# Expert bias moved into the expert tiles, PSUM banks dealt anew, and the end of an iteration reordered, in a fused two-layer transformer kernel

## The reference, cut to what matters

```
gate_logits = x @ W_gate;  top_w, top_idx = top_k(gate_logits, 2);  top_w = softmax(top_w)
combine = sum over k of one_hot(top_idx) * top_w
for e in range(8):
    h = gelu(x @ W_in[e] + b_in[e])
    y = h @ W_out[e] + b_out[e]
    out = out + combine[..., e, None] * y
x = layernorm(x + out)
```

## Time and profile before

| | |
|---|---|
| median of 3 runs | 1523.08 us (1520.47 to 1523.33) |
| profiled execution, own time | 1521.35 us |
| its span, first to last instruction | 1519.7 us |
| PE busy | 1297.7 us, 85% |
| DVE, ACT, POOL busy | 917.5, 650.7, 614.7 us |
| softmax attention | 0 to 587 us |
| iterations 0 and 1 | 587 to 656 us |
| iterations 2 to 8 | 656 to 1240 us, PE busy 540.0 |
| last iteration | 1240 to 1317 us, PE busy 46.6 |
| hand-over to the experts | 1317 to 1341 us |
| expert tiles | 1341 to 1481 us, PE busy 136.7 |
| final norm | 1481 to 1519.7 us |

### The profile page before, as it was taken

The page is one execution under the profiler, slowest core; times in us unless marked ns, Lnnn a source line. Parts: engine busy times, 40 slices in busy tenths (PEclk is TensorE's granted clock), DMA queues, the critical chain, the costliest instruction groups (busy, mean ns, idle before and its releaser), DMA issues. The chain is left out here.

```text
span 1519.7 us, 34060 instructions
## 1 busy us (share of the span) xinstructions
PE 1297.7 (85%) x10704; PEld 745.3 (49%) x10705; DVE 917.5 (60%) x2055; ACT 650.7 (43%) x1290; POOL 614.7 (40%) x655
## 2 busy tenths in 40 slices
PE   6699999899999985998989999998989885499990
PEld 4243333333333332346565565646565553389990
DVE  6778887688887672155645646565645636445445
ACT  4065555555555564242524333242415221155553
POOL 7123232223232232035362827264463728235556
PEclk9599999999999997999999999999999998689995
DMA  6351111111111103030302203040402122132225
GB/s 196 101 186 38 37 37 51 40 47 37 35 38 50 44 14 102 8 82 6 97 9 57 52 26 83 7 102 7 102 5 59 34 91 61 39 111 68 66 58 168
DMA packets 88046, 93.09 MB, mean 61 GB/s; under 512 B 17192, under 2 KB 72368, under 8 KB 87856
## 3 DMA queue, kind: packets, MB, share of 16 engines
q1 hardware_dynamic: 73232, 74.39, 17.8%
q0 software_dynamic: 9184, 13.39, 2.9%
q10 hardware_dynamic: 5568, 4.53, 0.9%
HBM read 49.32 MB, written 22.63 MB: 47 GB/s over the span
## 5 line engine op out<-in xcount | busy, mean ns | idle before, releaser
L1307 ACT ACTIVATE arena<-banks 128x512 f32<-128x512 f32 x576 | 302.4, 599 | 239.2 <-PE banks L1222 237.7
L1354 DVE TENSOR_REDUCE arena<-banks 128x4 f32<-128x512 f32 (+3 forms) x336 | 343.8, 1055 | 89.8 <-PE banks L1200 85.8
L413 PE MATMUL banks<-arena,h 128*128 128x512 f32 x512 | 227.3, 594 | 2.6 <-ACTq L361 1.0
L1197 PE MATMUL banks<-arena 96*128 96x512 bf16 (+3 forms) x768 | 209.0, 341 | 20.8 <-DVE arena L1354 14.4
L1222 PE MATMUL banks<-arena 99*128 99x512 bf16 (+3 forms) x768 | 175.8, 328 | 16.4 <-ACT arena L1307 11.3
L1475 POOL TENSOR_SCALAR_AFFINE_SELECT arena<-arena 128x512 f32<-128x512 f32 x128 | 79.9, 636 | 229.2 <-ACT arena L1307 229.2
L1247 PE MATMUL banks<-arena 128*32 128x512 f32 (+3 forms) x1536 | 156.8, 496 | 15.7 <-POOL arena L1475 15.6
L413 PEld LDWEIGHTS banks<-arena,h 128*128 128x128 f32 x512 | 94.7, 190 | 110.3 <-issue 106.3
L1197 PEld LDWEIGHTS banks<-arena 96*128 96x128 bf16 x768 | 68.0, 100 | 158.7 <-DVE arena L1354 115.9
L429 POOL TENSOR_TENSOR arena<-arena 128x4 f32<-128x4 f32 x24 | 24.5, 1019 | 290.7 <-DVE arena L427 290.7
L502 POOL TENSOR_TENSOR arena<-arena 128x1024 f32<-128x1024 f32 x40 | 100.1, 2508 | 82.2 <-DVE arena L500 82.2
(11 more groups left out here) (168 smaller groups left out, 2019.8 us busy)
## 6 DMA issues: line engine op xcount, KB each, us to landing
arena<-arena SPq DMA_DIRECT2D x160, 128.0 KB, 2.3
arena<-q_parts SPq DMA_DIRECT2D x96, 96.0 KB
arena<-k_parts SPq DMA_DIRECT2D x288, 32.0 KB
arena<-rows SPq DMA_DIRECT2D x72, 65.0 KB
arena<-best SPq DMA_DIRECT2D x16, 256.0 KB, 4.5
k_parts<-arena SPq DMA_DIRECT2D x24, 128.0 KB, 2.8
q_parts<-arena POOLq DMA_DIRECT2D x18, 128.0 KB, 2.9
arena<-in_xT SPq DMA_DIRECT2D x8, 256.0 KB, 4.3
```

What stands on the lines that cost most here:

```text
L413: ins = nc.tensor.matmul(dst, l, r, start=(n == 0), stop=(n == len(pairs) - 1), skip_group_check=True)
L1197: ins = nc.tensor.matmul(dst, sq[p][0:MROW, h, qt * P:(qt + 1) * P], sk[p][0:MROW, h, k0:k0 + n], start=True, stop=not diag, skip_group_ch ...
L1307: nc.scalar.activation(pe_[:, s % NSLOT, :], score[s % NBANK], ACT.Exp, scale=SCALE0)\
L1354: nc.vector.tensor_reduce(mx[:, 1 if k0 else 0, qt, hs[0]:hs[-1] + 1], src, AX.X, ALU.max)\
```

## The change

The diff does four things.

- The bias leaves the iteration: picked, comb, turn_w, turned_w, bias, start and `acc` go. x3 itself is stored to `rest_d` right behind norm 3, from ACT's queue. `b_dn` is now laid out over all partitions and loaded beside `w_in`, so that each expert has 512 + 128 columns. `take_w` copies all 640 of them, a new DVE step `weigh` (one tile ahead) multiplies the 128 bias columns by the token weights, and `take_y` becomes a scalar_tensor_tensor that adds this product. `take_w` and `take_y` wait for `s_bias` too.
- The banks of the linear attention: `attend` takes its two `got` banks first and its two `grown` banks behind them, and one bank is skipped before `scores1(0)`. Now pv1 takes banks 6 and 7, freed by the masks of step 1; pv2 banks 4 and 5, freed by the masks of step 2; pv3 banks 0 and 1, freed by state1; the scores of step 3 banks 2 and 3, freed by state0.
- The end of the iteration: tile2(3) comes ahead of `choose`, and `route` (count on PE, place to weight on DVE) comes behind norm 2 and ahead of the scatters. down0 holds bank 0, count bank 1.
- The start: turn2 comes behind m = 2 instead of m = 1, and silu no longer waits for the bias of the iteration before.

```diff
         res = view([P, B, P])
-        acc = view([P, B, P])
         gated = view([P, 2, 512])
-        hid = [view([P, 4, 512]) for _ in range(2)]
-        w_in = view([P, NE, 512])
+        hid_both = view([P, 8 * 512])
+        hid = [hid_both[:, 2048 * i:2048 * i + 2048].rearrange("p (k t) -> p k t", k=4) for i in range(2)]
+        w_in = view([P, NE, 512 + C])
         stats = view([P, B, 8])
...
+            def skip_bank(self):
+                self.held.append(self.held[len(self.held) - 8])
+
             def pad_banks(self):
                 while len(self.held) % 8:
-                    self.held.append(self.held[len(self.held) - 8])
+                    self.skip_bank()
...
             for m in range(4):
-                if m == 2:
+                if m == 3:
                     tp.part = "rear"
...
                     bk, late["w1"][:, m * P:(m + 1) * P], xt1, start=True, stop=True))
-                tp.do("act", f"silu{m}", [f"up_a{m}", f"mul{m - 2}" if m >= 2 else (f"mul{m + 2}", 1), ("bias", 1)],
+                tp.do("act", f"silu{m}", [f"up_a{m}", f"mul{m - 2}" if m >= 2 else (f"mul{m + 2}", 1)],
                       lambda: nc.scalar.activation(gated[:, m % 2, :], bk, ACT.Silu, scale=late["s1"][:, m:m + 1]))
...
                 pr, half = n % 2, n // 2
-                got, *grown, other = [tp.bank() for i in range(4)]
-                got = [got, other]
+                got, grown = ([tp.bank() for i in range(2)] for j in range(2))
                 assert grown[0][0] % 8 < 7
...
+            tp.skip_bank()
             scores1(0)
...
             tp.part = "rear"
-            layernorm(tp, 3, "res3_3", res, x3, [("scatter7", 1), ("start", 1)])
+            layernorm(tp, 3, "res3_3", res, x3, [("scatter7", 1), ("stored", 1)])
             tp.do("act", "x3_again", ["norm3", ("scatter7", 1)], lambda: nc.scalar.copy(x3_rows[:, 1, :, 0:C], x3))
+            tp.do("act", "stored", ["norm3"], lambda: nc.scalar.dma_start(
+                rest_d[bass.ds(c, 1)].rearrange("c p b k -> p (c b) k"), x3), line="out")
...
                     wgt[:, 1, :], wgt[:, 1, :], wgt[:, 0, :], ALU.mult))
-                tp.do("dve", "picked", ["second", "onehot"], lambda: last(nc.vector.tensor_tensor(
-                    pick[:, i, :, :], chosen[:, B * i:B * i + B, :],
-                    wgt[:, i, :].rearrange("p (b o) -> p b o", o=1).to_broadcast([P, B, 8]), ALU.mult)
-                    for i in range(2)))
-                tp.do("dve", "comb", ["picked", ("turn_w", 1)], lambda: nc.vector.tensor_tensor(
-                    comb, pick[:, 0, :, :], pick[:, 1, :, :], ALU.add))
...
             turned(tp, 3, x3, x3T, [("gate", 1), "up_b3"])
-            choose()
             tp.part = "front"
...
             tp.part = "rear"
-            route()
+            choose()
             tp.part = "pre"
...
             tp.part = "rear"
+            route()
             for g in range(TOPK * B):
...
                     in_=x3_rows[:, g // B, g % B, :], in_offset=None), line="scat", apart=(g == 0))
-
-
-            tp.part = "rear"
-            k, bk, fr = tp.bank()
-            tp.do("pe", "turn_w", ["comb"] + fr, lambda: last(nc.tensor.transpose(
-                bk[0:8, t * P:(t + 1) * P], comb[:, t, :], ident[:, :]) for t in range(B)))
-            tp.do("act", "turned_w", ["turn_w", ("bias", 1), "mul3"], lambda: nc.scalar.copy(combT[0:8, :], bk[0:8, :]))
-            tp.free(k, "turned_w")
-
-            k, bk, fr = tp.bank()
-            tp.do("pe", "bias", ["turned_w"] + fr, lambda: last(nc.tensor.matmul(
-                bk[:, t * P:(t + 1) * P], combT[0:8, t * P:(t + 1) * P], late["b_dn"][0:8, :], start=True, stop=True)
-                for t in range(B)))
-            tp.do("dve", "start", ["bias", ("stored", 1)], lambda: nc.vector.tensor_tensor(
-                acc, bk.rearrange("p (b c) -> p b c", b=B), x3, ALU.add))
-            tp.free(k, "start")
-            tp.do("act", "stored", ["start"], lambda: nc.scalar.dma_start(
-                rest_d[bass.ds(c, 1)].rearrange("c p b k -> p (c b) k"), acc), line="out")
             tp.pad_banks()
...
             if me == "sp":
-                nc.sync.dma_start(w_in, a["w_in"].rearrange("e p m -> p e m")).then_inc(s_experts, 16)
+                nc.sync.dma_start(w_in[:, :, 0:512], a["w_in"].rearrange("e p m -> p e m")).then_inc(s_experts, 16)
+                nc.sync.dma_start(w_in[:, :, 512:512 + C], a["b_dn"]).then_inc(s_experts, 16)
                 for g in range(NE):
...
             if me in ("pe", "dve"):
-                e.wait_ge(s_experts, 32)
+                e.wait_ge(s_experts, 48)
...
                 wait(s_up, XG * J + k - 3)
+                wait(s_bias, XG * J + k - 3)
                 nc.vector.tensor_copy(w_now[:, k % 4, :], w_in[:, bass.ds(x, 1), :].rearrange("p o m -> p (o m)"))\
...
                 e.wait_ge(s_down, XG * J + k + 1)
+                e.wait_ge(s_bias, XG * J + k + 1)
                 wait(s_back[k], 16 * J)
-                nc.vector.tensor_scalar(y_g[:, k, :], banks[:, 4 + k % 2, 0:P], x_g[:, k, C + 1:C + 2], None,
-                                        ALU.mult).then_inc(s_y, 1)
+                nc.vector.scalar_tensor_tensor(out=y_g[:, k, :], in0=banks[:, 4 + k % 2, 0:P],
+                                               scalar=x_g[:, k, C + 1:C + 2], in1=bias[:, k % 2, :],
+                                               op0=ALU.mult, op1=ALU.add).then_inc(s_y, 1)
+
+            def weigh(J, k):
+                e.wait_ge(s_xg[k], 16 * (J + 1))
+                e.wait_ge(s_w1, XG * J + k + 1)
+                wait(s_y, XG * J + k - 1)
+                nc.vector.tensor_scalar(bias[:, k % 2, :], w_now[:, k % 4, 512:512 + C], x_g[:, k, C + 1:C + 2], None, ALU.mult).then_inc(s_bias, 1)
...
             chain = {"sp": [(load, 0)], "pe": [(turn, 3), (up, 1), (down, 0)], "act": [(gelu, 0)],
-                     "dve": [(take_x, 3), (take_w, 2), (take_y, 0)], "pool": [(back, 0)]}[me]
+                     "dve": [(take_x, 3), (take_w, 2), (weigh, 1), (take_y, 0)], "pool": [(back, 0)]}[me]
             NJ = NTILE // XG
```

More of the change, by code:

```diff
@@ L88 @@
 LATE = ["wo0", "w1", "w2", "h12", "w3", "s1", "s2", "sh1", "sh2", "s3", "wq", "wk", "wv", "wo1", "wo1s",
-        "mask1", "qdec", "kdec", "bdec", "wgate", "b_in", "b_dn", "iota",
+        "mask1", "qdec", "kdec", "bdec", "wgate", "b_in", "iota",
         "before", "token", "region", "upto", "multiples", "number"]
@@ L267, in program @@
         sent = view([P, TOPK * B]).bitcast(U32)
-        pick = view([P, 2, B, 8])
-        comb = view([P, B, 8])
-        combT = gated[:, 0, :]
         idx8 = view([P, B, 8]).bitcast(U32)
@@ L277, in program @@
         b_in = late["b_in"][:, :].rearrange("p (e m) -> p e m", e=NE)
+        bias = gated[:, 0, 0:2 * C].rearrange("p (n c) -> p n c", n=2)
         reuse = carve(q_all.rearrange("p a b -> p (a b)"), 8 * 512)
@@ L288, in program @@
         STEPS_TAB = 16
-        w_now = hid[0][:, 0:4, :]
+        w_now = hid_both[:, 0:4 * (512 + C)].rearrange("p (k m) -> p k m", k=4)
         halves = [q_dec.rearrange("p a i b t -> p (a i b t)"), state.rearrange("p b i d -> p (b i d)"),
@@ L304, in program @@
         s_up, s_gelu = sem("s_up"), sem("s_gelu")
-        s_down, s_y = sem("s_down"), sem("s_y")
+        s_down, s_y, s_bias = sem("s_down"), sem("s_y"), sem("s_bias")
         s_back = [sem(f"s_back{k}") for k in range(XG)]
@@ L1541, in layouts @@
     a["w_dn"] = x["L1_ffn_W_out"].reshape(8, 4, P, C).transpose(0, 2, 1, 3)
-    a["b_dn"] = x["L1_ffn_b_out"]
+    a["b_dn"] = np.broadcast_to(x["L1_ffn_b_out"], (P, 8, C))
     p = np.arange(P)
```

## The result

The changed kernel takes 1527.78 us (median of 8 runs, 1526.85 to 1530.04); before, in the same comparison, 1521.64 (8 runs, 1520.47 to 1523.33). The ratio is 1.0040, 95% interval 1.0029 to 1.0051: about 6 us slower. 1515.4 had been forecast and 1523 was the end of the range, so the prediction was wrong in sign. The profiled execution has a span of 1526.8 us against 1519.7, and a mean granted clock of 0.941 against 0.949.

A forecast was written before the change was run, and what follows sets the result against it. TensorE, nearly without a break, was taken as the bound. Terms 6.4 - 0.9 + 1.9 + 0.8 + 0.5 - 0.7 - 0.3 gave 7.7 us off, so 1515.4 us from 1523.08; range 1510 to 1523.

The forecast's parts named there:

- the end of down0 to up_a1: End of an iteration: the wait for start becomes up_b0's wait for place, one matmul pair earlier; loss 0.41 us.
- Rival 4: Hand-over: the wait for place doesn't arise or costs nothing; 4 us better, 1511 us; chance 0.10.
- Expert tiles: 72 tiles with longer copy and weigh on DVE: PE stays the bound by a hair; 0.3 us lost in all.
- Rival 1: Expert tiles: DVE becomes the bound; 1526 us at 0.15 a tile, milder form 1521 at 0.08; chance 0.10 each.
- Swaps: Partition swaps before the first rotation: later scatters delay them, 0.1 us in each of seven iterations, 0.7 in all.
- rival 2: Partition swaps held up by scatters: 0.6 us in seven iterations, 4.2 instead of 0.7, giving 1519 us; chance 0.12.
- Hand-over to the experts: Between iterations and experts: paddings start earlier, scatters about 0.4 us earlier hold the fetch; gain 0.5 us.
- The attention's 1.5 us gaps: Linear attention: two PE gaps an iteration vanish, but PE then waits for POOL; gain taken as 0 of 3.0 us.
- rival 3: Linear attention: the gaps are really gained, 3.0 us in seven iterations, 21 us, giving 1494 us; chance 0.04.
- The last attention: Last iteration's attention: PE is late behind POOL there, so 0.8 us are gained once.
- Turn3 to down0's end: End of an iteration: reordered products fill PE's waits, 10.46 us becomes 8.98; gain 1.48 us, 1.9 in iteration 8.
- the forecast 83.2: Loop over column blocks: the period after the change in us, near 83.2 instead of 84.3.

The follow-up runs named there:

- the filled wait: Changed kernel plus twelve matmuls with unread results between up_a0 and up_b0, the wait for place kept: 1522.53 us, ratio 0.9996 to the kernel before.
- The count in another bank: Changed kernel with six banks skipped, so count takes bank 7 and up_b0 no longer waits for place: 1501.42 us, ratio 0.9859 to before.
- the tiles without the late ones: Tiles of the kernel before given only the new attention banks and one skipped bank: 137.97 us first to last take_y; kernel 1513.58 us, ratio 0.9942.
- the last one: Changed kernel with route ahead of norm 2, take_w copying 512 columns and weigh reading w_in directly into four buffers: 1495.14 us, ratio 0.9821 to before.
- the one with the padding: Kernel before with the new attention banks and seven skipped banks ahead of y, which dealt y a bank state3 frees: 1547.49 us, ratio 1.0169.

## Why the prediction was wrong

**The step that failed** is the one from the end of down0 to up_a1: "Loss 0.41 us. What is late next is nothing beyond PE." The wait was right to a tenth: `up_b0` was forecast 4.92 us behind down0's end and starts 4.86 behind it, held by `place` behind norm 2. With the clock kept, the loss is the forecast one, 0.35 us (the filled wait shows it). But I costed the wait as idle time only. The removed products, which I had counted only as time saved, were the work that lay between the waits; without them PE has two waits of 0.56 and 2.78 us with one pair of matmuls between, and in six of seven hand-overs the granted clock fell to the lower level for the products that followed. That is 12.0 us where nothing stood in the sum. The filled wait shows it by keeping the wait and removing the fall. (It shows that work in the wait keeps the clock; that the bias products did so before, rather than the shorter waits around them, is argued.) It also shows that 2.3 of the 12 would go back into longer swap stretches. 1527.8 less 9.7 is 1518.1 (an estimate): faster than before, so the fall turns the sign, but not the forecast 1515.4. It lies 2.7 us above that: the swaps and the tiles cost more than forecast, and the larger gain up to down0's end offsets only part of it.

A rule bears on this that the prediction did not weigh. The Trainium skill, TensorE: Matmul & The Clock Gate, "A second HAM failure mode: psum-queue depth-cycling", tells of a kernel whose short idle stretches between groups of matmuls were enough to make the granted clock swing. The trace agrees: 0.56 and 2.78 us idle with one pair between, and 1.91 us for a pair of 1.02.

**Rival 4** (the wait for `place` costs nothing) was mis-sized with it: it credited only 0.41 us an iteration. The count in another bank takes the hand-over from 11.06 to 8.36, 2.7 us, since the bias products' own time then is gained too. At 1501.4 us that case lies outside my range.

**Expert tiles**: forecast 0.3 us, measured 2.8 against the profile of before and 5.7 against the tiles without the late ones. I had the addition (0.33 to 0.46 against a slack of 0.43) and took it that PE stays the bound. The copy took 0.49 to 0.56 (once 0.70) where 0.50 to 0.54 was allowed for, `weigh` took 0.27 to 0.29 in 62 tiles and 0.40 to 0.48 in the other ten, and DVE is last in about every second tile. Rival 1 in its milder form held (0.08 us a tile), but it came with another loss that I did not have.

**Swaps**: forecast 0.1 us in each of seven iterations, measured 1.8 in all. Where every clock was kept, in the filled wait, it is 4.1, which is what rival 2 had priced (4.2): the slow hand-overs hid it. The first full iteration, which has no scatters ahead of it, keeps its 24.7 us in every kernel except the last one (25.65) and the one with the padding (26.67), neither of them explained; the others lengthen by up to 1.1 when the scatters start right ahead of the first projection, and by 0.3 from the third on with the scatters earlier. In the changed kernel the length goes by the hand-over ahead of it: behind 14.1 and 14.0 us it is 24.66 and 24.64, behind 13.0 it is 25.19 and behind 13.1 twice 24.9, behind the undisturbed 11.4 it is 25.56. This speaks for the scatters, but no run took them alone away, so it stays argued.

**Hand-over to the experts**: forecast 0.5 gained, measured 0.1 lost. The paddings do leave earlier, and the first scatter starts 6.51 us behind the gate product instead of 6.82, as forecast (this iteration has no norm 2 to stand behind). But the second and third scatter take 1.15 and 1.27 us where they took 0.96, so the last one starts 15.97 behind the gate product instead of 15.83. What lengthens them was not tested.

**What held.** The attention's 1.5 us gaps were worth nothing, because POOL's stream sets `grow3`: 0.08 us an iteration measured where 0 was taken, alone in the kernel before 0.07 (rival 3 fell). The last attention gained 0.77 (forecast 0.8). Turn3 to down0's end gained 1.74 us (forecast 1.48), in iteration 8 1.85 (1.9). The one middle iteration whose hand-over kept its clock has a period of 82.9 us, beside the forecast 83.2; the others run 84.8 to 85.6. That it comes out below 83.2 is luck: its swap stretch is a short one (24.64), behind a slow hand-over. In the filled wait, where every iteration kept its clock, the middle periods are 83.55 to 83.67.

## What to carry to other kernels

Before a product is removed because it is cheap to do without, look at what stands on both sides of it: between two waits it may be what keeps TensorE at its higher clock, and then the price of its removal is paid by the matmuls behind the second wait. Where banks are dealt in turn, find out for each moved step who frees the bank at the wrap-around and what stands ahead of that step in its engine's queue; putting `route` ahead of norm 2, with the order that this needs, made 0.4% slower into 1.5% faster, and six skipped banks alone made it 1.4% faster. An engine with a slack of 0.4 us per tile that is given 0.4 us is to be taken for the new bound.

## What the runs showed of the hardware that had not been expected

- PE's granted clock fell after 2.70 to 2.79 us without work in six of seven hand-overs (1.6 to 2.7 us lost each), and after 2.28 us in four of seven iterations of the padded kernel (1.6 us each). It did not fall behind the 1.03 us of before, nor behind the two waits of 1.5 us in its attention (clock 1.00 over the whole iteration), nor with twelve matmuls (2.75 us of work) in the gap. Hand-overs with the same instructions and the same idle time went either way, and no run shows what decides between them.
- A DVE copy of 128x640 takes 0.49 to 0.57 us (single ones 0.68 and 0.70), and up to 0.93 when POOL has a product of its own beside its scatter issue. The Trainium skill, SBUF — State Buffer, "Who interferes with whom", says that such a copy and GpSimd shut each other out, whoever comes first holding the other up for its whole instruction. The trace agrees in so far as it is DVE that was held here; I had weighed the rule only in the other direction.
